# Three transformer layers and a rotation on one core: MLP hidden layer in halves of 256 tokens, input loaded batch by batch, and engine queues ordered by the longest remaining chain

## What is computed

```
mod = silu(c) @ w_ada + b_ada                      # six rows of 288 for each batch
h   = modulate(layernorm(x), shift, scale)
q, k, v = split(h @ w_qkv + b_qkv)                 # 16 heads of 18
x  += gate * (attention(q, k, v) @ w_proj + b_proj)
h   = modulate(layernorm(x), shift_mlp, scale_mlp)
x  += gate_mlp * (gelu(h @ w1 + b1) @ w2 + b2)     # hidden size 1152
...
U = qr(P)[0];  R = expm(skew(silu(c) @ W.T + b))   # one 64 x 64 rotation for each batch
x + ((x @ U) @ R - x @ U) @ U.T
```

## Time and profile before

| what | value |
|---|---|
| time, 3 runs | median 1450.6 us (1448.38 to 1451.12) |
| profiled execution: its own time | 1447.77 us |
| profiled execution: span from first to last instruction | 1446.0 us |
| mean granted TensorE clock | 0.967 of full speed |
| TensorE matmul busy | 1337.2 us (92% of the span) |
| VectorE, ScalarE, GpSimd busy | 902.2, 788.8, 419.1 us |
| mean DMA rate | 63 GB/s over the span |

### The profile page before, as it was taken

The page is one execution under the profiler, slowest core; times in us unless marked ns, Lnnn a source line. Parts: engine busy times, 40 slices in busy tenths (PEclk is TensorE's granted clock), DMA queues, the critical chain, the costliest instruction groups (busy, mean ns, idle before and its releaser), DMA issues.

```text
span 1446.0 us, 30299 instructions
## 1 busy us (share of the span) xinstructions
PE 1337.2 (92%) x11841; PEld 813.3 (56%) x11841; DVE 902.2 (62%) x1985; ACT 788.8 (55%) x1563; POOL 419.1 (29%) x805
## 2 busy tenths in 40 slices
PE   2777999899999999999999999989999999999978
PEld 1444555556567565665655665546656565555545
DVE  4678776776855655575447564584858755766442
ACT  2466677566754534454435343465655775755622
POOL 1213243242431334323343233221313323231110
PEclk8787999999999999999999999999999999999989
DMA  5114224534212312132212213141000130000000
GB/s 156 46 37 143 75 76 157 153 122 141 80 31 73 73 51 81 25 64 85 81 40 55 77 42 122 58 92 51 1 13 6 30 88 5 22 10 22 14 25 17
DMA packets 76738, 91.80 MB, mean 63 GB/s; under 512 B 38989, under 2 KB 69814, under 8 KB 73270
## 3 DMA queue, kind: packets, MB, share of 16 engines
q1 hardware_dynamic: 74486, 87.52, 20.8%
q10 hardware_dynamic: 2112, 2.36, 0.6%
HBM read 73.22 MB, written 16.38 MB: 62 GB/s over the span
## 4 chain that ended last, share of the span: by engine, by line
PE 79%; DVE 6%; issue 5%; ACT 4%; DMA 3%; SPq 2%; POOL 1%; POOLq 0%; DVEq 0%; ACTq 0%
PE P L1389 33%; PE P L1549 7%; PE P L1550 7%; PE P L1551 7%; PE P L1518 4%; DVE NM L1819 3%; PE P L1509 2%; PE P L1566 2%; PE P L1416 2%; PE P L1485 2%; PE P L1406 2%; PE P L1494 1%; PE P L1546 1%; PE P L1472 1%; PE P L1560 1%
## 5 line engine op out<-in xcount | busy, mean ns | idle before, releaser
L1389 PE MATMUL P<-XT,W 128*128 128x512 f16 x1512 | 350.7, 383 | 7.6 <-DVE XT L1730 4.8
L2246 POOL TENSOR_TENSOR X<-X,TM 128x288 f32<-128x288 f32 x144 | 123.6, 860 | 532.6 <-DVE TM L1894 340.8
L1549 PE MATMUL P<-W,H 128*128 128x288 f16 x864 | 248.3, 287 | 0.4 <-issue 0.3
L1550 PE MATMUL P<-W,H 128*128 128x288 f16 x864 | 248.0, 287 | 0.0
L1551 PE MATMUL P<-W,H 128*128 128x288 f16 x864 | 248.0, 287 | 0.0
L1389 PEld LDWEIGHTS P<-XT,W 128*128 128x128 f16 x1512 | 141.3, 98 | 179.7 <-issue 22.8
L2165 ACT ACTIVATE G<-P 128x512 f32<-128x512 f32 x216 | 128.9, 597 | 140.5 <-PE P L1389 131.0
L2155 ACT ACTIVATE ARENA<-P 128x512 f32<-128x512 f32 x256 | 136.0, 599 | 102.8 <-PE P L1509 102.1
L1819 DVE TENSOR_REDUCE NM<-P 128x2 f16<-128x512 f32 x256 | 159.9, 687 | 11.1 <-PE P L1494 10.5
L1389 PE MATMUL P<-WQ,XT 128*128 128x288 f16 x1008 | 143.9, 295 | 10.2 <-issue 5.3
L1888 DVE TENSOR_TENSOR H<-G,H 128x512 f16<-128x512 f32 x139 | 97.9, 708 | 85.3 <-ACT H L2166 85.2
(11 more groups left out here) (306 smaller groups left out, 2170.2 us busy)
## 6 DMA issues: line engine op xcount, KB each, us to landing
W<-scr_w SPq DMA_DIRECT2D x9, 1440.0 KB, 6.1
W<-scr_w SPq DMA_DIRECT2D x9, 1368.0 KB, 5.8
scr_w<-W SPq DMA_DIRECT2D x4, 1440.0 KB, 5.7
scr_w<-W SPq DMA_DIRECT2D x4, 1368.0 KB, 5.7
STG<-in_L_w SPq DMA_DIRECT2D x8, 576.0 KB, 5.1
STG<-in_L_w SPq DMA_DIRECT2D x9, 432.0 KB, 4.5
STG<-in_L_WT SPq DMA_DIRECT2D x11, 324.0 KB, 4.3
G<-scr_ada SPq DMA_DIRECT2D x24, 144.0 KB, 3.6
```

The source lines that it names most:

```text
L1389: ins = e.matmul(o, l, r, start=k == 0, stop=k == len(pairs_) - 1)
L1549: e.matmul(o, hi, W2[:, 2 * m, :], start=False, stop=False)
L1550: e.matmul(o, hi, W2[:, 2 * m + 1, :], start=False, stop=False)
L2246: e.tensor_tensor(X[:, t, :], X[:, t, :], TM[st["k"]][:, :], ALU.add).then_inc(st.sem)
```

## The change

- The MLP keeps its pieces of two batches, but `up` goes batch by batch (v = 0, 1): each step takes two hidden blocks of 256 tokens, 14 matmuls of 256 columns into one bank (the ninth block alone, 7 matmuls). `H` becomes `[128, 2, 9, 2, 256]`, and each half has its own `h_rd`. `down` waits for blocks by fours. The batch becomes `ready` one at a time, and the last chunk of layer 2 (`SPLIT`) is made into two pieces, one for each batch.
- `x` is loaded batch by batch, 288 KB each: batch 0 from ScalarE's queue, 1 to 3 from SyncE's behind the first weights, the others when batch b-3 is prepared.
- The ones rows of `XT` and the fills of `V32` and `WP1` move from VectorE to GpSimd; `CS` and `PLUS` alone stay ahead of the first activation (`zeros`). The Householder steps are emitted only once batch 0 has its q and k.
- The planner takes DMAs as one wire of 270 KB a us with 1.6 us behind it, has other costs for the start, and `by_readiness` ranks steps that can begin by the longest chain of cost behind them, less a quarter of their old time.

```diff
...
 LAT, FILL, TAB = 0.08, 0.15, 1.3
-LANDS = dict(w_back=6.0, w_keep=5.8, g1_in=3.3, g2_in=4.0, x_in=7.5, w_in=5.0, w2_in=6.0, cond_in=5.0, tv_in=3.3)
+SIZES = dict(x_in=295, w_in=442, cond_in=345, w2_in=442, w_back=1400, w_keep=1400, g1_in=147, g2_in=295, tv_in=295, tv_out=295, out=295, v_in=640, wp1_in=350, p_in=74)
 AHEAD = 3
 NEAR = 0.1
+MIX = 0.25
+LATE = ("dconsts",)
 TABLES = dict(exps="exp", t_exp="exp", g_exp="exp", gelu="gelu", silu="silu")
+SPLIT = {(2, 3): [(0,), (1,)]}
...
+class Wire:
+
+
+    def __init__(self):
+        self.clock = 0.0
+
+    def land(self, kb, issue):
+        self.clock = max(self.clock, issue + 0.2) + kb / 270
+        return max(self.clock + 1.6, issue + 2.1)
...
+    for st in sorted(order, key=lambda st: -st.number):
+        st.rest = st.cost + max((x.rest for x in then.get(id(st), [])), default=0.0) + LAT + (st.kb / 270 + 1.6 if st.kb else 0.0)
+    for st in order:
+        st.index = -st.rest + MIX * st.begun
...
-        st.end = lane.clock + st.tail
+        st.end = lands(st, lane.clock)
...
-            st.end = lane.clock + (LANDS.get(kind, 2.2) if incs >= 16 else FILL if lane is pe else 0.0)
+            st.kb, st.lane = SIZES.get(kind, 8) if incs >= 16 else 0, lane
+            st.end = lands(st, lane.clock)
...
-        consts = do(pool, "consts", 8.0, incs=1)
-        xt_ones = do(dve, "xt_ones", 2.5)
-        dconsts = do(dve, "dconsts", 2.0, after=consts)
+        consts = do(pool, "consts", 3.2, incs=1)
+        zeros = do(dve, "zeros", 0.4)
+        xt_ones = do(pool, "xt_ones", 5.5, incs=7, after=consts)
+        dconsts = do(dve, "dconsts", 4.4, after=consts)
...
-        x_in = [do(act, "x_in", 0.1, incs=16, raises=f"x_in{q}", q=q) for q in range(4)]
-        for t in range(NT):
-            XW[t] = [x_in[t // 4]]
-        silu = do(act, "silu", 0.5, src=c_in, zero=xt_ones)
+
+        def x_load(lane, b):
+            if b < B and not XW[2 * b]:
+                XW[2 * b] = XW[2 * b + 1] = [do(lane, "x_in", 0.45, incs=16, raises=f"x_in{b}", b=b)]
+
+        x_load(act, 0)
+        silu = do(act, "silu", 0.5, src=c_in, zero=zeros)
...
+                x_load(sp, b + 3)
...
-            for m in range(9):
-                if not held and (len(acts) == AHEAD or not taken("gelu")):
-                    yield from hold("gelu")
-                    held = True
-                yield from slot(rP)
-                _, j, pf = rP.take()
-                mt = do(pe, "up_mm", mm_cost(7, 512), m=m, c=c, j=j, w=tok["w1"], x=xt, free=pf)
-                for _ in range(2 if len(acts) > 1 else 1):
-                    if lows:
-                        low()
-                    if acts and held:
-                        activate()
-                acts.append((m, j, mt))
-                yield "free"
+            for v in vs:
+                hw[v] = []
+                xt = [TW[t] for t in (4 * c + 2 * v, 4 * c + 2 * v + 1)]
+                for m in range(0, 9, 2):
+                    if not held and (len(acts) == AHEAD or not taken("gelu")):
+                        yield from hold("gelu")
+                        held = True
+                    yield from slot(rP)
+                    _, j, pf = rP.take()
+                    mt = do(pe, "up_mm", mm_cost(14 if m < 8 else 7, 256), v=v, m=m, c=c, j=j, w=tok["w1"], x=xt, free=pf)
+                    for _ in range(2 if len(acts) > 1 else 1):
+                        if lows:
+                            low()
+                        if acts and held:
+                            activate()
+                    acts.append((v, m, j, mt))
+                    yield "free"
+                for t in (4 * c + 2 * v, 4 * c + 2 * v + 1):
+                    TR[t] = TR[t] + [mt]
...
+        def down(L, e, c, vs):
...
                 yield from slot(rP)
                 _, j, pf = rP.take()
-                for g in range(3):
-                    mt = do(pe, "down_mm", mm_cost(9 + (g == 0), C), g=g, n=n, j=j, h=ht[3 * g:3 * g + 3], w=tok["w2"], free=pf)
+                for g, (a, z) in enumerate(((0, 4), (4, 8), (8, 9))):
+                    mt = do(pe, "down_mm", mm_cost(3 * (z - a) + (g == 0), C), a=a, z=z, n=n, j=j, h=ht[a // 2:(z + 1) // 2], w=tok["w2"], free=pf)
...
+                if n % 2:
+                    h_rd[v] = [mt]
+                    if not any((k, d) == (L, c) and v in some for k, _, d, some in ms.todo[1:]):
+                        flags.add(("x", L, t // 2))
...
         def householder():
+            while ("turned", 0, 0) not in tok:
+                yield "wait"
...
-                            self.todo.append((L, e, c))
+                            for vs in SPLIT.get((L, c), [(0, 1)]):
+                                self.todo.append((L, e, c, vs))
...
             def able(self):
-                return bool(self.todo) and "retired" in flags and (("ada", self.todo[0][0]), 5) in tok and self.todo[0][0::2] in self.ready
+                return bool(self.todo) and "retired" in flags and (("ada", self.todo[0][0]), 5) in tok and all((self.todo[0][0], 2 * self.todo[0][2] + v) in self.ready for v in self.todo[0][3])
...
-            h_rd[0] = rSTG.free[3:]
+            h_rd[0], h_rd[1] = rSTG.free[3:5], rSTG.free[5:]
...
+        x_load(sp, 1)
+        x_load(sp, 2)
...
             def up_mm(st):
-                m, c = st["m"], st["c"]
+                at = (2 * st["c"] + st["v"]) * 256
                 q.wait_ge(st["w"], st["x"], st["free"])
-                products(bank(st), [(W1[:, w, m * 128:(m + 1) * 128], XT[:, x, c * 512:(c + 1) * 512]) for x, w in PRODUCTS], st)
+                for k, m in enumerate(range(st["m"], min(st["m"] + 2, 9))):
+                    for i, (x, w) in enumerate(PRODUCTS):
+                        ins = e.matmul(bank(st)[:, 256 * k:256 * k + 256], W1[:, w, m * 128:(m + 1) * 128], XT[:, x, at:at + 256], start=i == 0, stop=i == 6)
+                ins.then_inc(st.sem)
 
...
-                e.memset(WP1[:, :, :], 0.0)
...
+            def xt_ones(st):
+                q.wait_ge(consts)
+                e.memset(XT[96:128, 2, :], 0.0).then_inc(st.sem)
+                q.wait_ge(st.at(1))
+                e.memset(XT[96:98, 2, :], 1.0).then_inc(st.sem)
+                q.wait_ge(st.at(2))
+                for i in range(2):
+                    e.memset(V32[i][:, :, :, :], 0.0).then_inc(st.sem)
+                q.wait_ge(st.at(4))
+                for i in range(2):
+                    e.memset(V32[i][:, :, :, 18:19], 1.0).then_inc(st.sem)
+                e.memset(WP1[:, :, :], 0.0).then_inc(st.sem)
+
...
```

154 lines of the change are left out of this document (82 added, 72 removed).

## The result

The change made the kernel faster: 1435.45 us (1433.05 to 1437.5, 4 runs) beside 1450.65 (1448.38 to 1451.12, 4 runs), ratio 0.9898 with a 95% interval of 0.9876 to 0.9919. That is 15 us, where 23.6 were forecast. The profiled execution of the changed kernel took 1437.0 by its own time, so between the two profiled executions lie only 10.7 us; places are read from these two, totals from the ratios.

The account below looks back on a forecast made before the run. TensorE bounds the kernel, its matmuls busy 1337 of 1446 us. Terms -20 - 9 + 5.4 + 0 = -23.6 take the profiled 1447.8 to 1424.2, median 1427; own range 1412 to 1440, 8 in 10 within 1404 to 1446.

Parts of the forecast that it names:

- likeliest case: Whole kernel: the forecast itself, a median of 1427 us, chance 0.57.
- Head, -20: Start up to the first projection: it begins at 21 to 22 instead of 41.91, 20 us earlier (bounds 10 to 24).
- It shifts as a whole: Stretch from 42 to 150 us: the chain of projection, maxima, scores moves earlier with the head, keeping the 20 us.
- rival B: From 42 to 150, weight conversions and DMAs set the first `up`; about 5 of the 20 us stay: 1442, chance 0.12.
- I cost that at nothing: Householder steps: they follow later, nobody needs their result before the rotation at the program's end; 0 us.
- Tail, -9: Batch 7's two layernorm stalls at the end, filled with batch 6's `up` and `down` matmuls: 9 us saved (4 to 10).
- Halves, +5.4: `up` as 3024 matmuls of 256 columns instead of 1512 of 512: 5.4 us more (0 to +8).
- Middle, 0 (-15 to +15): 150 to 1300 us: new queue order removes some small waits and adds others; net 0.
- A: Middle gains too: half its idle time goes and VectorE is free for maxima; another 17 us, 1410, chance 0.20.
- C: Slower: ScalarE waits at weight arrivals, 8.2 us each, passed on to TensorE; 1460 at four places, chance 0.10.
- D: `up`: the 1512 added weight loads are exposed, 69 ns each, +104 us, 1531, chance 0.01.

Follow-up runs that it names:

- head_only: Kernel before with only the new start (`x` batch by batch, fills on GpSimd, their planner costs), Householder steps still first: 1450.2 us, ratio 1.0015.
- head_hh: Kernel before with the new start and the late Householder steps; old rank, old DMA table, whole `up`: 1438.25 us, ratio 0.9922.
- old_rank: Changed kernel with the order of emission as rank again and no late `dconsts`, DMA model by size kept: 1436.28 us, ratio 0.9909.
- start_wire: Changed kernel without its halves and its new rank; new start, late Householder steps and DMA model kept: 1431.98 us, ratio 0.9892.
- split_up: Kernel before with each `up` step issued as 256-column products, same steps, order and waits: ratio 1.0036, +5.2 us (2.5 to 8.0).

## Why the prediction was right, and where it was not

The forecast was a gain of 23.6 us in the profile, 1427 for the median; it came to 15.2 by the medians and 10.7 in the profile. The sign, the range (1404 to 1446) and the likeliest case hold, in its own range of 1412 to 1440 too. Not all of the terms do.

- **Head, -20.** The moment is right (21.71), and the chain before it nearly to the microsecond. What failed is the step "It shifts as a whole". In the earlier trace rows the first 42 us held 13.2 us of work, mostly condition products, that in the change are still to be done after the projection has started. Moved forward were not 20 us but 23.8 - 13.2 = 10.6 us of work, and 3.9 more by 150 (8.5 and 13.5 in all if every product is counted at what it takes at the full clock). The chain itself did shift, so rival B's sign, a first `down` no earlier, did not come; rows of before, then of the change, for the first `up` and the first `down`:

```profile
165.11 1.67 PE L1389 MATMUL P<-XT,W 128*128 128x512 f16 x7
...
194.62 0.30 PE L1546 MATMUL P<-W,ONES 128*128 128x288 f16 x1
```

```profile
143.08 2.32 PE L1596 MATMUL P<-XT,W 128*128 128x256 f16 x10
...
179.59 0.28 PE L1603 MATMUL P<-W,ONES 128*128 128x288 f16 x1 [1.04 <-ACT H L2217]
```

`up` comes 22.0 us earlier and `down` 15.0. No run gives the head a single price: taken out of the change, the start costs 7.1 us and the late Householder steps 5.7; put into the kernel before, the two together win 11.3, with a projection at 31.2.
- **Householder steps, "I cost that at nothing".** Wrong: 13.5 us between head_only and head_hh, 5.7 in the change. The rotation does not wait for their result, but their small steps stand in the queues from 17 to 895 us, and TensorE can wait there for the next of them, as in old_rank at 926.
- **Tail, -9.** Right in place and near in size: 9.5 us of idle time, 7.6 of them in the two holes, which are covered by just the matmuls named. It hangs on the halves (start_wire still has both pauses), not on `SPLIT`. What it is worth to the total is another matter: start_wire, with both pauses, is as fast.
- **Halves, +5.4.** Right for what it prices: +5.2 by itself. But halves also rearrange the middle, by 12.5 us of idle time with the old DMA table, 7.4 with the new model, and nothing only with the new rank.
- **Middle, 0 (-15 to +15).** As idle time it came to -1.1. The net over the whole kernel hid two large terms of opposite signs: the DMA model, worth 10 with halves and 4 without, and a finer interleaving, which costs 12.6 of busy time with whole `up` and some 11 with halves. My ledger had idle time and slow clock as the only things that an order can change; the page could have warned me only after the change, by a busy time that rose by 13.9 where the halves explain 5.
- **Rivals.** A did not come: the total is above 1410, and the Householder steps gave their gain elsewhere. B's outcome holds for the start alone (+2.2), not for the whole. C did not come: ScalarE waits for weights to land 5.3 us once at the start, 4.2 at most after that, and not at all for layer 2's QKV weights. D is excluded by split_up.

So that the sum lies in its range is in part luck, by errors that cancelled: 9 too much in the head, nothing for the Householder steps and the DMA model, nothing for the breaks.

What stays open: whether the early Householder steps are what delays TensorE between 150 and 400, and by which queue; why the halves lose 12.5 us of idle time in the middle on the old table; what the late `dconsts` are worth apart from the rank; and whether a rank that counts a change of stream as a cost, with halves and DMA model, would keep the gains of both. That last version was not tried.

## What to carry to other kernels

When a chain is moved forward, count how much work is done by a fixed time before and after, not by how much the first product of the chain moves: here 10.6 us of 20. A new order of a queue changes busy time as well as idle time, by every break between streams of unlike shape; compare the busy time of the same instructions first. And take a bundle apart even if its total agrees with the forecast: of these parts one alone made the kernel 15.5 us slower and another alone won nothing, and three of them without the other two are as fast as all.

## What the runs showed of the hardware

- Behind a 512-column matmul of full shape (128*128) at the full clock, the next one started after 215 to 228 ns if it was of full shape too (1410 cases in the trace of before), and after 309 to 312 ns if it was not (79 cases). A finer interleaving with 122 more changes of shape cost 10.1 us.
- A pause of 2.96 us in dense work was followed by 10 us at a granted clock of 0.50, so that it cost about 8 us and not 3. Behind pauses of 3.16 us at 942 and 3.32 us at 1336 in the same trace it was 0.59 over 4 us and 0.50 over 6, so the price varies with the place.
